# Wo projection, ternary projection and the turning of the first batch's rows in one stage of 32 steps

## The reference, cut to what matters

```python
x = x + softmax_attention(layernorm(x)) @ Wo            # 32 heads of 16, 8 KV heads, causal, rotary
x = x + (layernorm(x) @ kernel + bias)                  # "ternary projection", 512 x 512
x = x + decay_attention(layernorm(x))                   # 32 heads of 128, linear attention with decay:
#   q, k, v = silu(h @ qkv_w.T); gate = sigmoid(h @ gate_w.T)
#   (gate * rmsnorm(attention) * norm_w) @ out_w.T
x = x + routed_ffn(layernorm(x))                        # 512 x 512, a low-rank part chosen by row
```

## Time and profile before

| | us |
|---|---|
| median of 3 runs | 3268.4 (3267.42 to 3271.03) |
| span of the profiled execution | 3264.1 |
| PE busy in the span | 3086.6 (95%) |
| DVE, ACT, POOL busy | 1298.5, 1324.3, 938.9 |

### The profile page before, as it was taken

The page is one execution under the profiler, slowest core; times in us unless marked ns, Lnnn a source line. Parts: engine busy times, 40 slices in busy tenths (PEclk is TensorE's granted clock), DMA queues, the critical chain, the costliest instruction groups (busy, mean ns, idle before and its releaser), DMA issues. The chain is left out here.

```text
span 3264.1 us, 52462 instructions
## 1 busy us (share of the span) xinstructions
PE 3086.6 (95%) x18776; PEld 2470.0 (76%) x18776; DVE 1298.5 (40%) x2268; ACT 1324.3 (41%) x2317; POOL 938.9 (29%) x746
## 2 busy tenths in 40 slices
PE   7699999887799999999999998999999999999978
PEld 5444444356688888888888887888888888888866
DVE  6677776626322222223222234223222232222258
ACT  4256666631343333433333343433333334333321
POOL 4411111102332332333233332333333333233221
PEclk9789999998899999999999998999999999999989
DMA  4411211000111111111111111111111111111101
GB/s 134 114 26 26 38 26 38 14 1 17 55 36 51 35 45 45 35 35 40 47 39 43 44 35 36 36 35 46 41 39 50 36 35 35 51 35 45 45 20 52
DMA packets 97286, 135.40 MB, mean 41 GB/s; under 512 B 23924, under 2 KB 44148, under 8 KB 97208
## 3 DMA queue, kind: packets, MB, share of 16 engines
q1 hardware_dynamic: 97208, 134.36, 14.3%
HBM read 121.87 MB, written 12.06 MB: 41 GB/s over the span
## 5 line engine op out<-in xcount | busy, mean ns | idle before, releaser
L1443 PE MATMUL bank<-l_xT_hi,l_w_T 128*128 128x512 f32 x3072 | 788.8, 399 | 0.0
L1443 PEld LDWEIGHTS bank<-l_xT_hi,l_w_T 128*128 128x128 f32 x3072 | 556.0, 188 | 104.0
L1373 DVE TENSOR_TENSOR l_sc<-bank,l_mask 128x512 f32<-128x512 f32 x128 | 88.6, 692 | 955.1 <-PE bank L1499 942.0
L1443 PE MATMUL bank<-l_xT_lo,l_w_T 128*128 128x512 f32 x1536 | 412.7, 390 | 0.0
L710 ACT ACTIVATE att_exp<-bank 128x512 f32<-128x512 f32 x576 | 322.5, 597 | 203.1 <-PE bank L803 196.3
L1240 POOL TENSOR_TENSOR l_w_T<-l_w_raw,l_w_T 128x512 fp32r<-128x512 f32 x198 | 255.6, 1292 | 513.2 <-ACT l_w_T L1285 513.1
L748 DVE TENSOR_REDUCE att_max<-bank 128x1 f32<-128x640 f32 (+6 forms) x352 | 345.9, 1025 | 107.3 <-PE bank L788 104.0
L1443 PEld LDWEIGHTS bank<-l_xT_lo,l_w_T 128*128 128x128 f32 x1536 | 288.4, 188 | 63.9
L1443 PE MATMUL bank<-l_o_T,l_y_hi 128*128 128x512 f32 x1024 | 324.1, 393 | 7.3 <-DVE l_y_lo L1345 7.3
L1443 PE MATMUL bank<-l_v_T,l_xT_hi 128*128 128x256 f32 x2048 | 295.0, 285 | 3.4 <-DVE l_xT_lo L1004 3.4
L1314 ACT ACTIVATE l_v<-bank 128x256 f32<-128x256 f32 x256 | 98.1, 383 | 492.6 <-PE bank L1443 492.6
(11 more groups left out here) (222 smaller groups left out, 4584.2 us busy)
## 6 DMA issues: line engine op xcount, KB each, us to landing
l_w_raw<-in_L_attn_qkv_w SPq DMA_DIRECT2D x198, 256.0 KB, 3.2
l_w_raw<-in_L_attn_gate_w SPq DMA_DIRECT2D x66, 256.0 KB, 2.6
l_o_raw<-in_L_attn_out_w SPq DMA_DIRECT2D x33, 512.0 KB, 3.6
query_parts<-att_exp SPq DMA_DIRECT2D x48, 128.0 KB
att_QT<-query_parts SPq DMA_DIRECT2D x16, 384.0 KB, 5.7
X<-in_L_attn_x SPq DMA_DIRECT2D x4, 1024.0 KB, 11.1
att_QT<-query_parts SPq DMA_DIRECT2D x16, 256.0 KB, 5.6
l_mask<-in_decay SPq DMA_DIRECT2D x32, 128.0 KB, 2.1
```

The lines of the kernel that those rows point to most:

```text
L1373: dve.tensor_tensor(sc[:, half(s)].rearrange("p (c n) -> p c n", n=P), ps_a[n % NA][:, :].rearrange("p (c n) -> p c n", n=P), mask[:, h, : ...
L1443: mm = pe.matmul(out, lhs, rhs, start=(n == 0), stop=(n == len(pairs) - 1))
```

## The change: what it does

One block, `project_and_turn`, takes the place of the two `project_tiles` blocks, of the credit block and of the first part of `linear_attend` for b = 0.

- Steps u = 0 to 15 are the Wo steps, u = 16 to 31 the ternary steps, in one pipeline: tiles are turned into the same two banks, multiplied into banks 6 and 7.
- `row_scales` makes 1/std and an offset -mean/std for eight tiles at a time; it is called three times (after DVE's steps 9 and 17 for the two halves of stats[0], after step 25 for the first half of stats[1]), each with one square root on ACT.
- Normalizing goes from DVE (`tensor_scalar`) to ACT (Identity with scale and bias taken from SBUF).
- POOL adds the bias to X as soon as the tile is normalized, ahead of the product's addition, not after it.
- The eight tiles of batch 0 are normalized, turned and split for the decay attention (index z below) by `TURN_AFTER`: one behind step 27, two behind each of steps 28 to 30, one behind step 31, through banks 2 to 5.
- The first eight weight tiles of the decay attention are loaded at the start of the block, cast on ACT in steps 2 to 9, their low parts made on POOL; the load of the first `o_raw` follows them. `linear_attend` for b = 0 then starts with its loop.
- POOL raises the 13 semaphores at the start of the block.
- The decay attention's buffers are placed over those of layer 0 (`Placed`), so that they exist while the block runs; kT and qd move among them.
- `normalize_transposed` (b = 1 alone now) makes the scales of its own eight tiles, not of 16.

```diff
+L1_FILLS = (("v", 0), ("v", 1), ("k", 0), ("q", 0), ("k", 1), ("g", 0), ("q", 1), ("g", 1))
...
+def row_scales(core, tag, stats, tiles):
...
+    def vector(dve):
+        dve.tensor_tensor(d, me, mo, ALU.subtract).then_inc(step, 1)
+        dve.tensor_tensor(both, me, mo, ALU.add).then_inc(step, 1)
+        dve.tensor_tensor(v, ve, vo, ALU.add).then_inc(step, 1)
...
+        dve.tensor_scalar(var, e, 1.0 / DIM, EPS, ALU.mult, ALU.add).then_inc(step, 1)
+        dve.wait_ge(root, 1)
+        dve.reciprocal(r, std).then_inc(step, 1)
...
+    def scalar(act):
+        act.wait_ge(step, 6)
+        nc.scalar.activation(std, var, ACT.Sqrt).then_inc(root, 1)
...
+def project_and_turn(nc, banks, X, O, wo, w_ffn0, bias, ident_f, stats, xT_hi, xT_lo, buffers, sems, credits, qkv_w, out_w,
+                     gate_w):
...
+        ROWS_A, ROWS_B, ROWS_Z = 9, 17, 25
+        TURN_AFTER = {27: (0,), 28: (1, 2), 29: (3, 4), 30: (5, 6), 31: (7,)}
...
+        ps_xT, ps_z, ps_y = banks[0:2], banks[2:6], banks[6:8]
...
+                sp.dma_start(bias_all[:, :], bias.unsqueeze(0).broadcast_to([P, DIM])).then_inc(bias_in, 16)
+                for n, (kind, h) in enumerate(L1_FILLS):
+                    if n >= RAW:
+                        gate(sp, fill_lo, n - RAW + 1, sp_passed)
...
+                    sp.dma_start(w_raw[:, n % RAW, :], src).then_inc(w_in[n % RAW], 16)
+                sp.dma_start(o_raw[:, :, :], out_w[0]).then_inc(o_in, 16)
...
+                for t in range(TILES):
+                    pool.wait_ge(normed, t + 1)
+                    nc.gpsimd.tensor_tensor(X[:, t, :], X[:, t, :], bias_all[:, :], ALU.add).then_inc(biased, 1)
...
+                def normalize(t):
+                    _, _, scaled, rstd, offset = halves[t // Z]
+                    act.wait_ge(scaled, 1)
+                    act.wait_ge(transposed, TILES + t - 1)
+                    nc.scalar.activation(xn[:, t % 2, :], X[:, t, :], ACT.Identity, bias=offset[:, t % Z:t % Z + 1],
+                                         scale=rstd[:, t % Z:t % Z + 1]).then_inc(normed, 1)
...
+                for u in range(U + 2):
+                    if u < U:
+                        high(u)
+                    if u == ROWS_A + 1:
+                        halves[0][1](act)
...
+                    if 2 <= u < 2 + len(L1_FILLS):
+                        keep_fill(u - 2)
+                    if TILES - 2 <= u < U - 2:
+                        normalize(u - TILES + 2)
+                    turned = TURN_AFTER.get(u - 2, ())
+                    for z in turned:
+                        high_z(z)
+                    if u == 28:
+                        normalize_z(0)
+                        normalize_z(1)
+                    for z in TURN_AFTER.get(u - 1, ()):
+                        if z >= 2:
+                            normalize_z(z)
...
+                for s in range(-1, U + 2):
+                    if s + 1 < U:
+                        low(s + 1)
+                    if 0 <= s - 1 < U:
+                        add(s - 1)
+                    if 0 <= s - 2 < U:
                         count(s - 2)
+                    if s == ROWS_A:
+                        dve.wait_ge(counted, Z)
+                        halves[0][0](dve)
...
+                    for z in TURN_AFTER.get(s - 1, ()):
+                        low_z(z)
...
+                for u in range(U):
+                    pe.wait_ge(lo_done, u + 1)
+                    if u >= 2:
+                        pe.wait_ge(added, u - 1)
...
+                    for x, w in passes((yT_hi, yT_lo), wo if u < TILES else w_ffn0):
...
+                    if u + 2 < U:
+                        transpose(u + 2)
+                    for z in TURN_AFTER.get(u, ()):
+                        transpose_z(z)
...
-                for n in range(ROW_FILLS if b == 0 else 0):
-                    keep_fill(n, 0)
-                n_scalar(act)
+                if b:
+                    n_scalar(act)
...
-                n_tensor(pe)
-                pe.wait_ge(lo_done, SEQ_TILES)
+                if b:
+                    n_tensor(pe)
+                    pe.wait_ge(lo_done, SEQ_TILES)
```

More of the change, by code:

```diff
@@ L84, in _, with __init__, sb @@
                     pool.sem_clear(sem)
+class Placed(Core):
+    def __init__(self, nc, ctx, start):
+        super().__init__(nc, ctx)
+        self.at = start
+    def sb(self, name, shape, dt=F32):
+        size = 2 if dt in (BF16, F16) else 4
+        for n in shape[1:]:
+            size *= n
+        at = self.at
+        self.at = at + (size + 31) // 32 * 32
+        return self.nc.alloc_sbuf_tensor_at(name, shape, dt, offset=at)
 CREDIT = 1
@@ new lines, in project_and_turn, with fill_target @@
+        z_normed = core.sem("mid_z_normed")
+        z_turned = core.sem("mid_z_turned")
+        z_hi = core.sem("mid_z_hi")
+        z_lo = core.sem("mid_z_lo")
+        halves = [row_scales(core, f"mid{h}", stats[0], slice(Z * h, Z * h + Z)) for h in range(BATCH)]
+        z_rows = row_scales(core, "midz", stats[1], slice(0, Z))
+        w_raw, o_raw, w_T, v_T = buffers[0:4]
+        w_in, o_in, fill_hi, fill_lo, sp_passed = sems[0], sems[1], sems[9], sems[10], sems[11]
+        def fill_target(n, part):
+            kind, h = L1_FILLS[n]
+            if kind == "v":
+                return v_T[part][:, :, h, :]
+            return w_T[part][:, "qkg".index(kind), h, :, :]
@@ L895, in _ @@
+                sp.dma_start(o_raw[:, :, :], out_w[0]).then_inc(o_in, 16)
             @block.gpsimd
             def _(pool):
[L897 to L902, removed]
+                for sem in credits:
+                    pool.sem_inc(sem, 1)
@@ L904, in _, with high @@
             @block.scalar
             def _(act):
[L906 to L912, removed]
+                def high(u):
+                    act.wait_ge(transposed, u + 1)
+                    if u >= 2:
+                        act.wait_ge(projected, u - 1)
+                    nc.scalar.copy(yT_hi[:, u % 2, :], ps_xT[u % 2][:, :]).then_inc(hi_done, 1)
@@ new lines, in normalize_z, with high_z @@
+                def normalize_z(z):
+                    _, _, scaled, rstd, offset = z_rows
+                    act.wait_ge(scaled, 1)
+                    if z >= 2:
+                        act.wait_ge(z_turned, z - 1)
+                    nc.scalar.activation(zn[:, z % 2, :], X[:, z, :], ACT.Identity, bias=offset[:, z:z + 1],
+                                         scale=rstd[:, z:z + 1]).then_inc(z_normed, 1)
+                def high_z(z):
+                    act.wait_ge(z_turned, z + 1)
+                    nc.scalar.copy(xT_hi[:, :, z * P:(z + 1) * P],
+                                   ps_z[z % 4][:, :].rearrange("p (c n) -> p c n", n=P)).then_inc(z_hi, 1)
@@ L914, in _ @@
             @block.vector
             def _(dve):
[L916 to L945, removed]
-                        count(s - 2)
+                def low(u):
+                    dve.wait_ge(hi_done, u + 1)
+                    if u >= 2:
+                        dve.wait_ge(projected, u - 1)
+                    dve.tensor_tensor(yT_lo[:, u % 2, :], ps_xT[u % 2][:, :], yT_hi[:, u % 2, :], ALU.subtract
+                                      ).then_inc(lo_done, 1)
@@ L959, in _ @@
[L959 to L964, removed]
+                        if u < TILES:
+                            src = O[:, KC * (t // Z) + c, t % Z, :]
+                        else:
+                            src = xn[:, t % 2, c * P:(c + 1) * P]
+                        mm = pe.transpose(ps_xT[u % 2][:, c * P:(c + 1) * P], src, ident_f[:, :])
@@ L1198, in load_raw, with load_weights @@
                     sp.dma_start(w_raw[:, n % RAW, :], src).then_inc(w_in[n % RAW], 16)
-                def load_weights(turn, before, first=False):
+                def load_weights(turn, before):
                     for n in range(ROW_FILLS):
```

227 lines of the change are left out of this document (143 added, 84 removed).

## The result

The changed kernel took 3228.9 us (median of 4 runs, 3227.58 to 3230.19) against 3269.72 for the kernel before on the same chip (3267.42 to 3271.26): ratio 0.988, 95% interval 0.9866 to 0.9894. The span of the profiled execution went from 3264.1 to 3228.2 us.

What follows compares the result with a forecast made beforehand. PE was taken as the bound, with time to gain in two holes around the ternary steps, where it stands or runs slowly. Span 3264.1 - 38.9 = 3225.2, plus 4.3 to the median: 3229.5, rounded 3230 us; range 3225 to 3242.

Steps and rivals of the forecast that it cites:

- the likeliest case: Whole kernel: the forecast itself, a median of 3225 to 3236 us, given a chance of 0.78.
- pace, step 1 to 14: Wo steps: 3.20 us each, set by PE; the ternary steps go no slower.
- joining, steps 16 to 18: Where Wo steps meet ternary steps: all 32 steps keep PE's pace of 3.20 us, if nothing else holds them.
- three chains of scales: Scales inside the pipeline: PE waits 0.3, 0.5 and 0.5 us, taken as 1.5, bounds 0 and 8.1.
- weights, first cast: Decay attention's first weights, loaded early: ACT wants the first in step 2, about 701 us; cost 0, 8 if late.
- turning seven tiles ahead of step 31: Batch 0's tiles turned in the last ternary steps: 7 x 0.4 = 2.8 us on PE.
- tail, from the start of step 31: End of the joined stage: from step 31's start to the end of the last sums, 5.4 us.
- Rival (a): Around the chains of scales DVE becomes the bound, chains unhidden and held by POOL: 3242 us; chance 0.12.
- Rival (b): In the joined stage ACT becomes the bound, by late weights (3238 us) or repeated table loads (3242); chance 0.06.
- Rival (c): PE's clock drops inside the stage, 1.9 us more a step, 3291 us if at all 32; chance 0.02.
- Rival (d): The hole only moves: PE waits at step 16 or in the loop as long as now, 3268 us; chance 0.02.
- launch and end: Outside the profiled span: the median of the runs lies 4.3 us above it, untouched by the change.

Runs made afterwards that it cites:

- the bias later: Against the changed kernel, POOL's bias additions to tiles 4 and 12 of the ternary half wait for the running chain of scales to end; 3225.06 us, one run.
- the halves apart: Changed kernel with its stage cut into two blocks behind step 15, both chains of stats[0] at the start of the second; 3237.78 us.
- the next batch: Changed kernel with batch 1's scales and turning moved into the tail of batch 0's block, first scale operations ahead of the loop; 3223.23 us.
- the changed kernel again: The changed kernel without any edit, measured and profiled a second time on another experiment's chip; 3230.3 us, ratio 0.9887 to the kernel before.
- the turning back: Changed kernel with scales and turning of batch 0 put back into the decay attention, weights staying ahead; 3245.54 us.
- both parts back: Changed kernel with both the first eight weight tiles and batch 0's scales and turning back in the decay attention; 3257.3 us.

## Why the prediction was right

The median was forecast at 3229.5, rounded 3230 us, and measured at 3228.9, inside the likeliest case's own range. That the two lie within a microsecond is partly luck, as the point on the span below shows; what bears the forecast out is the time from step 0 to the first product, 38.04 us less where the sum has 38.9. By the steps of the prediction:

| step | forecast, us | measured, us |
|---|---|---|
| pace, step 1 to 14 | 3.20 a step | 41.57 for 13 steps, 3.20 |
| joining, steps 16 to 18 | 3.20 each | 3.22, 3.18, 3.21 |
| three chains of scales | 0.3 + 0.5 + 0.5, taken as 1.5 | 0 + 1.05 + 1.06 = 2.1 |
| weights, first cast | at about 701, costs 0 | at 701.39, costs 0 |
| turning seven tiles ahead of step 31 | 2.8 | 2.95 |
| tail, from the start of step 31 | 5.4 | 5.5 (801.21 to 806.71) |
| block boundary | 0.6 | 0.67 (806.71 to 807.38) |
| step 0 to first product | 110.6 | 111.40 |
| first turn of heads | 72.6, as before | 72.37 |

- *The mechanism held.* The three undone parts are worth 11.65 us (weights), about 15.3 (scales and turning) and 9.07 (joining), 36.0 of the 38.04 us. The first two are taken to the first k product; the third is taken to the first product, since in that run the clock held behind it (to the first k product it is 7.57).
- *The term that was mis-sized is the chains,* 2.1 us where 1.5 was taken, and two errors partly cancel in it. Without POOL they cost less than forecast: the first nothing (its eleven operations took 2.2 us, 729.03 to 731.25, not 2.7, and the slack covered them), the others 0.27 each for ACT's order. POOL's hold of the last operation, which the prediction named and took as 0 with bounds of 0 and 1.3 a chain, cost PE 0.8 in each, 1.6 in all; the experiment with the bias later shows both sizes. The prediction's estimate by the Trainium skill's rule, 2.6, was nearer to that than the value taken. PE's waits came at steps 19 and 27, where the prediction lists 10, 18 and 26, and PE waits there for the DVE addition, as its working has it.
- *Rival (a)*, DVE as the bound, remained at two waits of 0.83 us. *Rival (b)* is out: the square-root table was loaded once ahead of the first chain (727.09 to 728.37, under DVE's low part and addition), and no Identity has a load beside it. *Rival (c)* is out for this execution: the clock was 1.00 from 700 to 808 us. Its price of 1.9 us a step was too low: in the step it was read from, the clock rose again (three groups of four matmuls took 2.07, 1.91 and 1.36 us, in the next step 1.17, 1.07 and 1.08). With the first group's loss in all three, a step at the lower clock would cost some 2.6 more, an estimate. *Rival (d)* is out by the trace.
- *The span fell by 35.9 us, not 38.9, and luck made it good in the median.* Step 0 came 2.94 us later than in the profile before and the start to the first product cost 0.8 more than forecast; the part behind the first product was 0.8 shorter (2420.8 against 2421.6). The first of these is layer 0, which the change leaves alone, and differs from one execution to the next: in the second profile of the same kernel step 0 lay at 693.68. So the span was 3228.2, 3.0 above the forecast 3225.2. Against that, the 4.3 us that the prediction adds as "launch and end" are not that. Wherever a run's time and span are both on record, they lie 1.7 to 2.2 us apart (3229.96 and 3228.2 in the profiled run of the changed kernel). The other 2.5 would be how far the profiled execution before lay below its median, since its own time is not on record. After, the median is only 0.7 above the profiled span, 3.6 less than was added. The two errors cancel. The median fell by 40.8 us, 2.8 more than the trace shows between the marks; that rest was not placed.
- *The clock at the first turn of heads* was forecast as low, with up to 1.9 us if it held. It was low in the first profile (0.79 over the first 8 us) and held in the second, worth 1.49 us.

## What to carry to other kernels

Before a chain of small operations is joined into a pipeline, look up what every other engine starts at its end: here the slack hid all of a chain of 2.2 us, and one addition on POOL, released by the normalizing that ACT does right behind the chain's square root, cost PE 0.8 us in each of the two others. Work that is written one behind the other on an engine, as the casts ahead of the square root here, adds up when it is moved out, so here each part could be priced alone, to about a microsecond. When a kernel's runs differ by more than the step that is argued about, compare stretches from a mark inside the trace and not the spans.

## What was not expected of the hardware

- The granted clock after a pause of PE is not settled by the pause: with 2.74 to 2.75 us of standing ahead of the first product it fell in one profile and held in four (the halves apart, the bias later, the next batch, the changed kernel again). The same is seen at step 0, whose first four matmuls took 2.07 or 2.08 us in eight of these profiles and 1.19 or 1.20 in three (the turning back, the next batch, the changed kernel again). In the two profiles of the changed kernel, 5.8 us apart (3228.2 and 3222.4), these two places make 1.43 and 1.49, and the start of step 0 another 2.30. What decides it stays open. At step 0 the profiles show where the low stretch went:

```profile
687.01 3.65 PE L838 MATMUL bank<-att_exp,V_columns 128*32 128x512 f32 x40
```

```profile
683.56 4.78 PE L838 MATMUL bank<-att_exp,V_columns 128*32 128x512 f32 x40
```

  These are the last 40 matmuls with V of the attention ahead of step 0, in the changed kernel's first profile and in its second. They took 3.65 us in all eight profiles with step 0 at the lower clock, and 4.75 to 4.78 in the three with step 0 at the full one; the granted clock from 10 to 5 us ahead of step 0 was 1.00 in the eight and 0.78 in the three. So a fast step 0 is not 1.43 us won: at least 1.1 of them are lost just ahead of the mark, where a stretch that starts at step 0 doesn't show them.
- Not every DVE operation that meets work of POOL is held by it. POOL's timeline with both parts back, beside DVE's above:

```profile
813.93 1.26 POOL L1383 TENSOR_TENSOR l_w_T<-l_w_raw,l_w_T 128x512 fp32r<-128x512 f32 x1 [0.30 <-ACT l_w_T L1428]
815.13 0.95 POOL L1388 MEMSET l_sq_sum<- 128x1024 f32 x1
816.02 3.51 POOL L1392 MEMSET l_acc<- 128x4096 f32 x1
```

  DVE's `tensor_tensor` at 814.30 took 0.91 us, until POOL's subtraction ended (815.19); the next one, at 815.25, took 0.17 in the middle of a clearing; the `tensor_scalar` at 815.45 took 4.14, until the second clearing ended. The kernel before shows the same three (0.86, 0.18 and 4.13 us from 823.62, 824.51 and 824.72), and with the turning back a `tensor_scalar` took 4.18 beside the two clearings, a `tensor_tensor` just ahead of it 0.17. In these rows an operation with two SBUF inputs was held by one of POOL that reads SBUF (here, and 0.17 to 1.24 us beside the bias) and not by a clearing, which reads nothing, and a `tensor_scalar` was held by a clearing. No run varied the operations one at a time.
